# Two graph layers on one core: layer 2's input turned by the transposing DMA, and the end of a group's TensorE order changed

## The reference

```python
# layer 0: 12 heads of width 64
h = einsum('bnd,ade->bane', x, W); th = tanh(h)
attn = th @ w_src + swap(th @ w_dst); attn = leaky(attn, 0.2)
attn = softmax(where(~adj, -999, attn)); f = elu(swap(attn @ h + b))
gate = sigmoid(x @ H_w.T + H_b); x = layernorm(x + gate * f + (1 - gate) * x)
# layer 1: 6 heads of width 128
q, k, v = heads(x @ Wq + bq), heads(x @ Wk + bk), heads(x @ Wv + bv)
p = softmax(q @ k.T / sqrt(128) + where(adj, 0, -9e15))
x = layernorm(x + heads_joined(p @ v) @ Wf + bf)
```

## Time and profile before

| | us |
|---|---|
| median of 3 runs | 2831.16 |
| lowest, highest | 2830.09, 2835.73 |
| profiled execution, its own time | 2832.2 |
| its span | 2830.5 |
| TensorE busy in the span | 2779.6 |
| DVE busy | 1719.1 |
| ACT busy | 1174.0 |
| GpSimd busy | 564.0 |

### The profile page before, as it was taken

The page is one execution under the profiler, slowest core; times in us unless marked ns, Lnnn a source line. Parts: engine busy times, 40 slices in busy tenths (PEclk is TensorE's granted clock), DMA queues, the critical chain, the costliest instruction groups (busy, mean ns, idle before and its releaser), DMA issues.

```text
span 2830.5 us, 51601 instructions
## 1 busy us (share of the span) xinstructions
PE 2779.6 (98%) x21342; PEld 2560.2 (90%) x21342; DVE 1719.1 (61%) x3334; ACT 1174.0 (41%) x2659; POOL 564.0 (20%) x326
## 2 busy tenths in 40 slices
PE   8999999999999899999999999999999999999998
PEld 6777778778777789999999999999999999999998
DVE  6899998889888655444445444444544444444443
ACT  5667776666666532322332232222332223223322
POOL 1322222222221121212221121212121221112120
PEclk9999999999999999999999999999999999999999
DMA  5556655555555421112111211111111221121110
GB/s 180 158 136 158 161 149 141 133 138 141 138 140 135 158 68 57 46 53 67 62 46 46 68 58 56 46 59 66 57 46 46 68 68 46 46 68 57 57 35 23
DMA packets 214379, 246.27 MB, mean 87 GB/s; under 512 B 135297, under 2 KB 151681, under 8 KB 214145
## 3 DMA queue, kind: packets, MB, share of 16 engines
q1 hardware_dynamic: 214144, 242.98, 29.7%
HBM read 142.65 MB, written 75.89 MB: 77 GB/s over the span
## 4 chain that ended last, share of the span: by engine, by line
PE 72%; DVE 16%; DMA 9%; issue 2%; SPq 1%; ACT 0%; DVEq 0%
PE ps_k L70 15%; PE ps_a L1091 14%; PE ps_q L70 14%; PE ps_a L70 14%; PE ps_hg L942 6%; DMA dst_all<-dst_scratch 6%; DVE logits L674 3%; DMA dst_scratch<-dst 2%; PE ps_s L1041 2%; PE ps_c L1073 2%; DVE logits L681 2%; DVE dst L698 2%; DVE dst_all L694 2%; DVE logits L677 2%; DVE neg_max L686 2%
## 5 line engine op out<-in xcount | busy, mean ns | idle before, releaser
L942 PE MATMUL ps_hg<-w_hi,xT 128*128 128x512 f32 x2268 | 747.6, 402 | 12.9 <-DVE h_one L714 12.5
L942 PEld LDWEIGHTS ps_hg<-w_hi,xT 128*128 128x128 f32 x2268 | 427.8, 189 | 120.1 <-issue 17.1
L942 PE MATMUL ps_hg<-w_lo,xT 128*128 128x512 f32 x1134 | 449.7, 397 | 0.0
L563 ACT ACTIVATE qT<-ps_q,bq_col 128x256 f32<-128x256 f32 x192 | 80.5, 470 | 666.0 <-PE ps_q L70 666.0
L70 PE MATMUL ps_k<-x1T_hi,wk_hi 128*128 128x256 f32 x1152 | 328.8, 285 | 0.0
L70 PE MATMUL ps_q<-x1T_hi,wq_hi 128*128 128x256 f32 x1152 | 321.8, 279 | 1.4 <-DVE x1T_lo L817 1.4
L70 PE MATMUL ps_k<-x1T_lo,wk_hi 128*128 128x256 f32 x1152 | 321.8, 279 | 0.0
L70 PE MATMUL ps_q<-x1T_lo,wq_hi 128*128 128x256 f32 x1152 | 321.5, 279 | 0.0
L70 PE MATMUL ps_q<-x1T_hi,wq_lo 128*128 128x256 f32 x1152 | 321.5, 279 | 0.0
L70 PE MATMUL ps_k<-x1T_hi,wk_lo 128*128 128x256 f32 x1152 | 321.4, 279 | 0.0
L1091 PE MATMUL ps_a<-wf_hi,cT_hi 128*128 128x384 f32 x768 | 265.4, 346 | 2.4 <-DVE wf_lo L286 2.4
(11 more groups left out here) (137 smaller groups left out, 5468.9 us busy)
## 6 DMA issues: line engine op xcount, KB each, us to landing
x_tok<-x SPq DMA_DIRECT2D x64, 384.0 KB, 3.9
dst_all<-dst_scratch SPq DMA_DIRECT2D x128, 192.0 KB, 3.4
gate_scratch<-gate SPq DMA_DIRECT2D x64, 384.0 KB, 2.5
feat_scratch<-feat SPq DMA_DIRECT2D x128, 192.0 KB, 2.8
feat_in<-feat_scratch SPq DMA_DIRECT2D x62, 384.0 KB, 3.1
gate_in<-gate_scratch SPq DMA_DIRECT2D x62, 384.0 KB, 3.7
x_even<-x SPq DMA_DIRECT2D x16, 768.0 KB, 4.3
x_odd<-x SPq DMA_DIRECT2D x16, 768.0 KB, 4.5
```

Of the source, the lines that this page charges most:

```text
L563: act.activation(dst_[h], ps[:, h * GN:(h + 1) * GN], ACT.Identity, bias=col[:, a:a + 1]).then_inc(signal, 1)
L942: ins = pe.matmul(ps_hg[:, cols], left[a][c], right[b][c], start=(c == 0 and n == 0), stop=(c == KC - 1 and n == 2))
```

## The change

For the groups from G = BY_DMA = 2 on, the input is no longer transposed by TensorE. GpSimd copies each tile of x1_tok into two planes of uint16 (`split_x1`), SP issues one transposing DMA a tile (`turn_x1`), GpSimd joins the turned planes to float32 words with two copies a tile (`join_x1`), ACT rounds and DVE takes the rest, now from SBUF. The planes share bytes with feat_in and gate_in, the turned planes with x1T_hi, the joined words with x1T_lo. So the DMA waits for the value products of the group before (v_done), and the loads of feat_in and gate_in wait for the DMA. GpSimd's bias additions come after the splits and before the joins. DVE's `rest_x1` for these groups comes after the second output addition. In all groups, the context blocks of pairs 1 and 2 are reordered: five blocks that don't need the last value product, then the three that do; and the output products 0 and 1 are computed chunk pair by chunk pair in turns (`last_contexts`, `first_outputs`).

```diff
+    BY_DMA = 2
+        x1T_raw = at(S + 6144, "x1T_raw", [P, KC, GN])
+        planes1T = at(S, "planes1T", [P, GT, 2, D], U16)
+        planes1 = at(S + 24512, "planes1", [P, GT, 2, D], U16)
+        def turn_of(G, t):
+            return GT * (G - BY_DMA) + t + 1
@@ sync
+            def turn_x1(G, t):
+                sp.wait_ge(split1_done, turn_of(G, t))
+                sp.wait_ge(v_done, 2 * GT * G)
+                sp.dma_start_transpose(planes1T[:, t].rearrange("p h (c n) -> p (h c) n", n=P),
+                                       planes1[:, t].rearrange("p h (c d) -> p (h c) d", d=P)).then_inc(turned1[t], 16)
             for G in range(NG):
                 s = G % 2
+                if BY_DMA <= G + 1 < NG:
+                    for t in range(GT):
+                        turn_x1(G + 1, t)
                 if G + 2 < NG:
                     sp.wait_ge(mixed, GT * (G + 2))
+                    if G + 1 >= BY_DMA:
+                        for t in range(GT):
+                            sp.wait_ge(turned1[t], 16 * (G + 2 - BY_DMA))
                     feat_and_gate(G + 2, 0)
@@ gpsimd
+            def split_x1(G, t):
+                pool.wait_ge(x1_ready, GT * G + t + 1)
+                pool.tensor_copy(planes1[:, t], x1_tok[G % 2][:, t, :].bitcast(U16).rearrange("p (d h) -> p h d", h=2)
+                                 ).then_inc(split1_done, 1)
+            def join_x1(G, t):
+                pool.wait_ge(turned1[t], 16 * (G + 1 - BY_DMA))
+                raw = x1T_raw[:, :, t * P:(t + 1) * P].bitcast(U16).rearrange("p c (n h) -> p h c n", h=2)
+                for h in range(2):
+                    ins = pool.tensor_copy(raw[:, h], planes1T[:, t, h].rearrange("p (c n) -> p c n", n=P))
+                ins.then_inc(joined1, 1)
             for G in range(NG):
                 s = G % 2
-                pool.wait_ge(x1T_done, 3 * (G + 1))
+                if G < BY_DMA:
+                    pool.wait_ge(x1T_done, 3 * (G + 1))
+                else:
+                    for t in range(GT):
+                        split_x1(G, t)
                 for t in range(GT):
+                    if G >= BY_DMA:
+                        pool.wait_ge(split1_done, turn_of(G, t))
                     pool.tensor_tensor(x1_tok[s][:, t, :], x1_tok[s][:, t, :], bf_all[:, :], ALU.add).then_inc(biased, 1)
+                if G >= BY_DMA:
+                    for t in range(GT):
+                        join_x1(G, t)
@@ scalar, round_x1: for G >= BY_DMA
+                        act.wait_ge(joined1, turn_of(G, GT - 1))
+                        src_ = x1T_raw[:, 2 * n:2 * n + 2, :]
@@ vector
-                if G + 1 < NG:
+                if G + 1 < BY_DMA:
                     rest_x1(G + 1)
...
                     ins = dve.bn_stats(stats[:, t, n % 2, :], x_)
+                    if n == 1 and BY_DMA <= G + 1 < NG:
+                        rest_x1(G + 1)
@@ tensor
+            def last_contexts(G):
+                probs_copied(G, 1)
+                pe.wait_ge(c_lo, 2 * (PAIRS * G + 1))
+                pe.wait_ge(v_copied, 2 * GT * G + 3)
+                for h, t in ((0, 0), (0, 1), (1, 0)):
+                    context_of(G, 1, h, t)
+                probs_copied(G, 2)
+                for h in range(2):
+                    context_of(G, 2, h, 0)
+                pe.wait_ge(v_copied, 2 * GT * (G + 1))
+                context_of(G, 1, 1, 1).then_inc(c_done, 1)
+                for h in range(2):
+                    ins = context_of(G, 2, h, 1)
+                ins.then_inc(c_done, 1)
+            def first_outputs(G):
+                if G == 0:
+                    pe.wait_ge(w1_ready, 4 * KC)
+                for j in range(PAIRS):
+                    pe.wait_ge(c_lo, 2 * (PAIRS * G + j + 1))
+                    for n in range(2):
+                        for c in (2 * j, 2 * j + 1):
+                            ins = output_chunk(n, c)
+                        if j == PAIRS - 1:
+                            ins.then_inc(o_done, 1)
+            def output(G, n):
+                if n == 3:
+                    pe.wait_ge(o_added, 2 * GT * G + 1)
@@ tensor, the group loop
-                context(G, 0)
+                first_context(G)
                 transpose_probs1(G, 2)
                 value(G, 3)
-                if G + 1 < NG:
+                if G + 1 < BY_DMA:
                     transpose_x1(G + 1)
-                context(G, 1)
-                context(G, 2)
-                for n in range(2 * GT):
+                last_contexts(G)
+                first_outputs(G)
+                for n in range(2, 2 * GT):
                     output(G, n)
```

More of the change, by code:

```diff
@@ L233, in two_graph_layers @@
         x1T_done, x1hi_done, x1lo_done = (sem(n) for n in ("x1T_done", "x1hi_done", "x1lo_done"))
+        split1_done, joined1 = (sem(n) for n in ("split1_done", "joined1"))
+        turned1 = [sem(f"turned1_{t}") for t in range(GT)]
         v_done, v_copied, o_done, o_added = (sem(n) for n in ("v_done", "v_copied", "o_done", "o_added"))
@@ L555, in round_x1 @@
                 for n in range(3):
-                    act.wait_ge(x1T_done, 3 * G + n + 1)
-                    act.copy(x1T_hi[:, 2 * n:2 * n + 2, :],
-                             ps_x[n][:, :].rearrange("p (c n) -> p c n", c=2)).then_inc(x1hi_done, 1)
+                    if G < BY_DMA:
+                        act.wait_ge(x1T_done, 3 * G + n + 1)
+                        src_ = ps_x[n][:, :].rearrange("p (c n) -> p c n", c=2)
+                    else:
+                        act.wait_ge(joined1, turn_of(G, GT - 1))
+                        src_ = x1T_raw[:, 2 * n:2 * n + 2, :]
+                    act.copy(x1T_hi[:, 2 * n:2 * n + 2, :], src_).then_inc(x1hi_done, 1)
             def heads_out(dst_, ps, col, j, signal):
@@ L816, in rest_x1 @@
                     dve.wait_ge(x1hi_done, 3 * G + n + 1)
-                    dve.tensor_tensor(x1T_lo[:, 2 * n:2 * n + 2, :],
-                                      ps_x[n][:, :].rearrange("p (c n) -> p c n", c=2),
+                    src_ = (ps_x[n][:, :].rearrange("p (c n) -> p c n", c=2) if G < BY_DMA
+                            else x1T_raw[:, 2 * n:2 * n + 2, :])
+                    dve.tensor_tensor(x1T_lo[:, 2 * n:2 * n + 2, :], src_,
                                       x1T_hi[:, 2 * n:2 * n + 2, :].bitcast(F32), ALU.subtract).then_inc(x1lo_done, 1)
@@ L1062, in value, with context_of, probs_copied @@
                         weights(wv_hi, wv_lo, slice((n % 2) * HALF, (n % 2 + 1) * HALF))).then_inc(v_done, 1)
-            def context(G, j):
+            def context_of(G, j, h, t):
+                a = 2 * j + h
+                return pe.matmul(ps_ctx[j][:, h * GN + t * P:h * GN + (t + 1) * P], v_tok[:, t, a * E1:(a + 1) * E1],
+                                 probs1T[:, (G + j) % 2, h * GT + t, :], start=True, stop=True)
+            def probs_copied(G, j):
                 pe.wait_ge(ptc_act, 2 * (PAIRS * G + j + 1))
@@ L1066, in context, with first_context @@
                 pe.wait_ge(ptc_dve, 2 * (PAIRS * G + j + 1))
-                pe.wait_ge(v_copied, 2 * GT * G + (2 if j == 0 else 4))
-                if j == 1:
-                    pe.wait_ge(c_lo, 2 * (PAIRS * G + 1))
+            def first_context(G):
+                probs_copied(G, 0)
+                pe.wait_ge(v_copied, 2 * GT * G + 2)
                 for h in range(2):
                     for t in range(GT):
[L1072 to L1075, removed]
+                        ins = context_of(G, 0, h, t)
@@ L1076, in context @@
                 ins.then_inc(c_done, 1)
-            def output(G, n):
+            def last_contexts(G):
[12 more added lines that the diff above has]
+                ins.then_inc(c_done, 1)
@@ L1079, in output, with output_chunk @@
+            def output_chunk(n, c):
+                left = nodes(cT, n // 2)
+                right = weights(wf_hi, wf_lo, slice((n % 2) * HALF, (n % 2 + 1) * HALF))
+                for k, (a, b) in enumerate(((0, 0), (0, 1), (1, 0))):
+                    ins = pe.matmul(ps_a[o_bank[n]][:, 0:HALF], left[a][c], right[b][c],
+                                    start=(c == 0 and k == 0), stop=(c == KC - 1 and k == 2))
+                return ins
+            def first_outputs(G):
                 if G == 0:
@@ L1080, in output @@
                     pe.wait_ge(w1_ready, 4 * KC)
-                if n < 3:
-                    pe.wait_ge(v_copied, 2 * GT * G + n + 2)
-                else:
+                for j in range(PAIRS):
[5 more added lines that the diff above has]
+                            ins.then_inc(o_done, 1)
@@ L1084, in output @@
+            def output(G, n):
+                if n == 3:
                     pe.wait_ge(o_added, 2 * GT * G + 1)
-                left = nodes(cT, n // 2)
-                right = weights(wf_hi, wf_lo, slice((n % 2) * HALF, (n % 2 + 1) * HALF))
                 for c in range(KC):
[L1088 to L1092, removed]
```

(1 more changed line is left out.)

## The result

The changed kernel took 2785.68 us (median of 4 runs, 2782.90 to 2787.47) against 2832.40 for the kernel before in the same runs: a ratio of 0.9833, 95% interval 0.9817 to 0.9848, 46.7 us less. That is inside the range given (2785 to 2812), at its lower edge. It is rival B's time (2785.5, chance 0.15), not the forecast's (2800), and it is outside the forecast's own narrow range (2792 to 2808). The way it went was right; one term of the sum was wrong.

What follows compares the result with a forecast made beforehand. TensorE was taken to bound layer 2. Transposes -39.3, the exposed copy wait +13.8, the last group -0.5 and interleaved outputs -5.3 gave -31.3 us: 2800 us forecast, own range 2792 to 2808, wider range 2785 to 2812.

Steps and rivals of the forecast that it cites:

- rival B: The wait for the last value copy costs nothing, ACT's copy being done when five context blocks are: 2785.5 us, chance 0.15.
- What bounds the kernel: In layer 2 TensorE, busy 98% of the span: a microsecond off it is one off the end, unless it then waits.
- Part 1: Twelve transposes leave TensorE's chain in each of 30 groups, 1.31 us each: -39.3 us, if the input arrives in time.
- Part 2: The DMA-turned input is ready 2.9 us before the next query product needs it, 2.3 with slow joins; TensorE doesn't wait.
- Part 3: Without transposes, contexts wait openly for ACT's last value copy: 0.46 us a group, +13.8 us; the last group gains 0.5.
- the price of the bare wait: TensorE's loss at the contexts when nothing hides ACT's last value copy: 1.0 us, seen in the last group.
- The cover: Five context blocks put before the wait for the last value copy hide 0.55 us of it, 0.11 a block.
- The bounds given: Limits for the open wait for the last value copy: nothing if the blocks cover more, 1.0 us if they cover nothing.
- Part 4: Interleaving output products 0 and 1 covers the wait for c_lo of pair 1: 0.17 us in 31 groups, -5.3 us.

## Why the prediction was right, and where it was not

- What bounds the kernel: right. A microsecond off PE's chain was one off the end: periods 1.53 us shorter, 46 us in 30 groups.
- Part 1, 1.31 us of transposes in 30 groups: right; the chain shows them gone whole. The Trainium skill's rule on transposes ("VectorE: DVE Perf Modes", "Rules for kernel authors"), TensorE where PSUM will do, did not bind: with 3.6 to 5.8 us a landing, twelve blocks at a time, the slower path lay wholly beside PE.
- Part 2, the input arrives in time with 2.9 us to spare: right (2.8 in most groups, 1.9 in the tightest), and that the margin is real is shown by the doubled and tripled joins.
- Part 3, the step that failed: the price of the bare wait, 1.0 us, was right (+1.01 when the old contexts came back). The cover was mis-sized: 0.55 forecast, 1.11 in fact, since an "x8" of instructions was read as eight blocks. The bounds given (nothing if the blocks cover more) and rival B had the true case, at a chance of 0.15. The remaining +13.8 of the sum did not exist, and the last group gained 1.0, not 0.5. Three blocks ahead left 0.23 open; the forecast's count would have left 0.67.
- Part 4, 0.17 us a group of c_lo: right. With the order alone the outputs went from 12.87 and 12.65 to 12.72 and 12.48, and the periods fell by 0.14. The same miscount stands in it, without harm: the two blocks behind pair 1's signal are 0.45 us and not 0.22, so the wait is covered by 0.7 and not 0.5.
- Not in the sum: the slower outputs of every second group are gone, 0.22 in 15 groups, 3 us; whether the edit does that isn't shown. And group 0 is 1.5 us shorter in its outputs, because PE stood idle only 0.8 us before them instead of 2.4. The chain there before and after, and the window of the changed kernel from 1022 to 1024, where the granted clock is 1.00 and not 0.58 as in the earlier trace rows:

```profile
1022.03 14.31 PE ps_a L1091 x72
```

```profile
1021.31 12.76 PE ps_a L1150 x72
```

```profile
1022.00:1024.00 2.00, 2.00 (x13) 2.00 (x12) 2.00 (x5) 1.32 (x4) 0.97 (x1) 1.00 0.00 0
```

This comes and goes with the execution and is not the edit's doing. The kernel with doubled joins has the same group 0, and there PE is idle for 2.4 us and the outputs take 14.32. In the traces of the kernels that keep the transposes of group 0, the pause is the short one where GpSimd's first addition starts after DVE's second wf_lo subtraction, and a longer one where it starts before.

The terms again: -39.3, with +0 for part 3 and -1.0 in the last group, -5.3, -3 and -1.5 give -50; 1.5 us come back as slightly longer key and query products (4.44 and 4.24 for 4.40 and 4.20). The spans differ by 49.6 us, the medians by 46.7. So the measured time is inside the range because the range took in rival B; that it comes within 0.2 us of B's 2785.5 is luck, since 3 and 1.5 us that nobody forecast are part of it.

## What to carry to other kernels

When work leaves the bounding engine, ask what it was hiding there: here the transposes hid a copy of 1.0 us, and moving them without reordering was worth 4 us instead of 47. Before a count in a row is divided by, it is to be matched with the loops of the code; one matrix product may be several instructions. A chain of four engines may be put beside a full one if its end and its deadline are added up; and the margin can be measured by doubling one of its links.

## What the runs showed that was not expected

The output product's matmuls run at one of two steps, about 173 ns or 176.5 ns, and keep it for all 72 of a group: 12.49 against 12.72 us without any wait, at a granted clock of 1.00. In the one trace of the kernel before it changes from group to group, in the changed kernel (two traces) and with old contexts it is always the short one, with three blocks ahead it was the long one in every group of one run and in some groups of the next. It does not hang on the transposes (the DMA alone has both too), nor on DMA traffic in that stretch: both steps occur with the DMA engines 0 to 1% busy (order alone) and with 45 to 46% (three blocks ahead). What sets it was not found.
